# A message-passing kernel on Trainium2: POOL scatters three edge groups in a row, then gathers for all three

## The reference

```python
row, col = (edge_index[0], edge_index[1])            # src, dst; the edges are sorted by dst
edge_input = jnp.concatenate([x[row], x[col], edge_attr], axis=-1)
h = jax.nn.silu(edge_input @ eW1 + eb1)
m_ij = jax.nn.silu(h @ eW2 + eb2)
agg = jax.ops.segment_sum(m_ij, row, num_segments=x.shape[0])
node_input = jnp.concatenate([x, agg], axis=-1)
update = jax.nn.silu(node_input @ nW1 + nb1) @ nW2 + nb2
...
x = _layernorm(x + (x + update), axis=-1)
```

## Time and profile before

| what | us |
|---|---|
| median of 3 runs | 1586.3 (1585.7 to 1588.1) |
| the profiled execution, its own time | 1574.37 |
| its span | 1572.9 |
| POOL busy, of it scatters L540 (391) and gathers L497 (391) | 1041.8; 387.9 and 397.9 |
| PE busy | 1207.4 |
| DVE busy | 761.0 |
| ACT busy | 459.5 |
| DMA, moved in all | 352.94 MB, mean 224 GB/s |

### The profile page before, as it was taken

The page is one execution under the profiler, slowest core; times in us unless marked ns, Lnnn a source line. Parts: engine busy times, 40 slices in busy tenths (PEclk is TensorE's granted clock), DMA queues, the critical chain, the costliest instruction groups (busy, mean ns, idle before and its releaser), DMA issues.

```text
span 1572.9 us, 24119 instructions
## 1 busy us (share of the span) xinstructions
PE 1207.4 (77%) x6825; PEld 865.5 (55%) x6825; DVE 761.0 (48%) x2819; ACT 459.5 (29%) x846; POOL 1041.8 (66%) x1267
## 2 busy tenths in 40 slices
PE   3812677788787888878888877777778979999994
PEld 3711354555554555545545454544445569888884
DVE  8940343443434434344343333333333449888885
ACT  0000111222222222222222222211212247777774
POOL 8877466556565565555656565666566548999996
PEclk9985799899999999998999898989889889999998
DMA  9995444456666666566656556555545259999994
GB/s 376 410 408 204 123 126 140 145 172 200 183 185 190 186 195 182 186 192 181 192 177 200 170 172 183 172 172 172 165 147 176 62 197 410 412 412 413 410 408 167
DMA packets 175498, 352.94 MB, mean 224 GB/s; under 512 B 30350, under 2 KB 81855, under 8 KB 175364
## 3 DMA queue, kind: packets, MB, share of 16 engines
q1 hardware_dynamic: 128740, 230.97, 44.6%
q10 hardware_dynamic: 21600, 68.32, 10.9%
q0 software_dynamic: 25024, 52.10, 10.5%
HBM read 235.21 MB, written 116.06 MB: 223 GB/s over the span
## 4 chain that ended last, share of the span: by engine, by line
PE 35%; issue 23%; another core or an unknown queue 17%; POOL 12%; DVE 8%; SPq 2%; DMA 2%; POOLq 0%; ACT 0%; DVEq 0%
PE psum L659 10%; POOL windows L614 6%; PE psum L703 5%; PE psum L682 4%; PE psum L705 4%; PE psum L701 3%; PE psum L690 3%; PE psum L715 3%; PE psum L647 2%; DVE same L994 2%; DVE work L988 2%; DVE work L978 2%; POOL windows L594 2%; POOL windows L603 2%
## 5 line engine op out<-in xcount | busy, mean ns | idle before, releaser
L540 POOL DMA_INDIRECT table<-qs,pos x391 | 387.9, 992 | 346.9 <-DVE qs L1022 250.0
L497 POOL DMA_INDIRECT ring<-x_d,idx_src x391 | 397.9, 1018 | 128.0 <-issue 118.5
L659 PE MATMUL psum<-work,windows 128*128 128x128 f32 x1568 | 235.8, 314 | 158.7 <-issue 158.7
L659 PEld LDWEIGHTS psum<-work,windows 128*128 128x128 f32 x1568 | 224.8, 225 | 227.9 <-issue 227.9
L978 DVE COPY work<-psum 128x512 f32<-128x512 f32 x98 | 67.8, 692 | 515.6 <-remote 322.4
L733 PE MATMUL psum<-work,ring 128*128 128x80 f32 x1250 | 156.8, 280 | 27.6 <-DVE work L1042 24.1
L733 PEld LDWEIGHTS psum<-work,ring 128*128 128x128 f32 x1250 | 148.7, 195 | 37.1 <-issue 20.1
L703 PE MATMUL psum<-work,w_src 128*128 128x512 f32 x196 | 117.9, 685 | 48.3 <-DVE work L978 45.5
L1022 DVE COPY qs<-psum 128x512 f32<-128x512 f32 x98 | 67.6, 689 | 161.4 <-remote 150.7
L682 PE MATMUL psum<-xT_in,w_self 128*128 128x320 f32 x314 | 126.5, 487 | 24.8 <-issue 19.1
L785 ACT COPY u_out<-psum 128x320 f32<-128x320 f32 x129 | 55.0, 426 | 295.3 <-remote 250.6
(11 more groups left out here) (121 smaller groups left out, 1613.3 us busy)
## 6 DMA issues: line engine op xcount, KB each, us to landing
windows<-x_d SPq DMA_DIRECT2D x392, 128.0 KB
ring<-table SPq DMA_DIRECT2D x79, 528.0 KB, 11.0
table<-empty ACTq DMA_DIRECT2D x9, 4224.0 KB
edge_rows<-edges_dram SPq DMA_DIRECT2D x98, 384.0 KB
xT_in<-xT_d SPq DMA_DIRECT2D x78, 320.0 KB
out<-windows ACTq DMA_DIRECT2D x78, 320.0 KB, 6.1
u_dram<-u_out SPq DMA_DIRECT2D x64, 320.0 KB
own_x<-x_d SPq DMA_DIRECT2D x48, 320.0 KB, 8.5
```

The lines of the kernel that those rows point to most:

```text
L497: pool.indirect_dma_start(rows, None, x[:, :], bass.IndirectOffsetOnAxis(ap=idx[:, g * TILES + t:g * TILES + t + 1], axis=0)).then_inc(don ...
L540: pool.indirect_dma_start(table[:, :], bass.IndirectOffsetOnAxis(ap=pos[:, g * TILES + t:g * TILES + t + 1], axis=0), q[g % Q][:, t, :], None,
L659: last = nc.tensor.matmul(p_dst[:, t * P:(t + 1) * P], window[g % WINDOWS][:, t, r * D:(r + 1) * D], pick[g % 2][:, r, t * P:(t + 1) * P], ...
```

## The change

POOL's loop over groups goes in turns of TURN = 3: it scatters the three groups of the turn one after the other and then gathers all that is owed for the three. The condition of each scatter and each gather, their number and their buffers stay as they are. The other branch (`pool.Else()`), which runs for other inputs, is not touched.

```diff
 LEAD, SHORT = X_SRC + 2, 6
+TURN = 3
...
                 pool.wait_ge(s_fill, 16 * len(FILL_BLOCKS))
-                for g in range(GROUPS):
-                    scatter(g)
-                    for h in range(gathered_by(g, LEAD), gathered_by(g + 1, LEAD)):
+                for g in range(0, GROUPS, TURN):
+                    turn_end = min(g + TURN, GROUPS)
+                    for h in range(g, turn_end):
+                        scatter(h)
+                    for h in range(gathered_by(g, LEAD), gathered_by(turn_end, LEAD)):
                         gather_src(h)
```

## The result

| what | before | after |
|---|---|---|
| median of 4 runs each, us | 1586.0 (1572.4 to 1588.1) | 1621.8 (1620.2 to 1622.7) |
| ratio, 95% interval | | 1.0258 (1.0222 to 1.0294) |
| the profiled execution, us | 1574.37 | 1622.43 |
| span, us; mean granted clock of TensorE | 1572.9; 0.914 | 1621.0; 0.883 |

The change costs 2.6%. On the medians that is +35.8 us, on the two profiled executions +48.1 us; the difference is that the profiled execution of before stood 11.9 us under its median and that of after stands at its own.

What follows compares the result with a forecast made beforehand. It took the loop to be bound by waits, PE's signals being held while POOL issues gathers. Early turns +18, late +26, last +1 made +45 us: 1619 for the profiled execution, 1631 us on the median's scale, range 1568 to 1675.

Steps and rivals of the forecast that it cites:

- What bounds the kernel: Edge loop: PE's signals reach DVE late while POOL issues gathers, let through about 1.5 us after it stops.
- The rule set against it: On-chip memory: PE and ACT never wait, DMA never contends with compute engines; POOL's DMA order would change the time by 0.
- The first interval of a turn: POOL's burst of scatters and gathers plus 2.4 us idle: 17.4 us early; 19.9 + 2.4 us late.
- The second interval: Four scatters alone after PE's long stall: 9.0 us early, 11.0 us late, between bounds 7.3 and 13.08.
- The third interval: The last group of a turn, at full clock: 7.3 us.
- The sum: Turns of 33.7 us early (+18 in all) and 40.6 late (+26), +1 for the last gathering turn: +45 us.
- its signs of being right: Bursts of 14.9 and 19.9 us, 2.4 us idle, q copied 1.5 us after, low clock, late turns losing over half.
- The saving: Per turn, one burst's end of 2.4 us is paid instead of two; the clock takes it back.
- Faster: q gets through inside the new burst: turns of 31.9 us early, 37.0 late, about -25 us, 1561 us; chance 0.20.
- No change: The hold costs 5.1 us per gathered group however grouped, or POOL's order matters to no one: 1586 us; chance 0.12.
- Much slower: The hold grows with the run of gathers, 3 us more per turn: +90 on the forecast, 1720 us; chance 0.08.
- Late gathers: In four late turns PE waits for gathers, if the hold does not cover it: +26 us, 1657 us; chance 0.10.

Runs made afterwards that it cites:

- experiment 1: Kernel before, with the gathers of the edge loop left out (messages of groups 28 to 97 wrong): 1264.4 us in one run.
- experiment 4: Kernel before, but in each group POOL waits for q, then issues the gathers owed, then the scatters: 1566.5 us, ratio 0.9893.
- experiment 7: Changed kernel with one added wait: after a turn's first gathered group POOL waits for PE's next q matmuls: 1577.2 us, ratio 0.9987.
- experiment 11: Kernel before, with gathers spread tile by tile, three or four per group, after PE's q matmul signal and ahead of the scatters: 1508.4 us, ratio 0.9537.
- experiment 10: Changed kernel's order, turns of three, with POOL issuing plain DMAs of the same size in place of the loop's gathers: 1309.8 us in one run.
- experiment 2: Kernel before, with the edge loop's gathers replaced by plain DMAs of the same size issued by SP: 1304.7 us in one run.
- experiment 3: Kernel before, with the edge loop's gathers replaced by plain DMAs of the same size issued by POOL at the same places: 1268.2 us in one run.
- experiment 6: Changed kernel with the gathers kept nine groups ahead instead of six (SHORT = 9): 1621.7 us, ratio 1.0261.

## Why the prediction was right, and where its terms were off

The forecast was slower, 1631 us; 1621.8 was measured. By its own steps:

*What bounds the kernel.* Right for the loop. The length of POOL's unbroken work on indirect DMAs sets the period: shown by experiments 1, 4, 7 and 11, and experiment 10 shows that plain DMAs in their place don't hold. The 11 scatters at the kernel's end are an exception that the prediction doesn't cover. The rule set against it, in the Trainium skill's SBUF — State Buffer (Who interferes with whom), nearly holds for what it names, the traffic: 40 us of 320 with SP's loads (experiment 2), 4 with POOL's (experiment 3). It does not cover the signals: q is copied 9.9 us after PE has it.

*The first interval of a turn.* 17.4 us forecast early, 17.93 measured; 22.3 forecast late, 22.54 measured. The burst was as worked out, 14.9 and 19.9 us; the idle time behind it is 3.2 and 3.7 us in the turns shown and not 2.4, because PE's signals come 2.2 us after the end of a burst of 12 and not 1.5. The lower clock isn't needed for it: behind the burst that ends at 482.08 us the clock was full (PEclk 1.00), and POOL idled as long,

```profile
482.08:485.27 3.19, 1.36 (x4) 0.29 (x2) 0.93 (x3) 0.86 (x2) 0.00 (x1) 1.00 0.17 48
```

```profile
485.28 0.99 POOL L541 DMA_INDIRECT table<-qs,pos  x1 [3.19 <-DVE qs L1025]
```

What sets the 2.2 us stays open.

*The second interval.* 9.0 early and 11.0 late were forecast, 7.92 and 9.06 measured. The late value was midway to the 13.08 us of the earlier trace rows, and that was a mis-reading: the interval from 1039.61 us is not four scatters alone, it has a burst of 8,

```profile
1044.80 0.99 POOL L497 DMA_INDIRECT ring<-x_d,idx_src  x1 [0.30 <-issue]
```

until 1049.56 us, so it shows a gathering group and says nothing on the clock's price for four scatters. The clock does fall, on the mean for 4.4 us of this interval early and 6.3 us late. The longest, 11.3 us, came once.

*The third interval.* 7.3 us was forecast as PE's own pace; 8.06 early and 8.22 late were measured. This step was mis-read too. PE's own pace with the node part is 8.21 us, as experiment 1 shows with no gathers at all; the 7.32 us in the earlier trace rows is, as I read it, a group in which PE had work done ahead during the hold.

*The sum.* A turn of 33.9 us early (746.0 / 22) against 33.7 forecast, 39.8 late (318.6 / 8) against 40.6: +23 and +19 us where +18 and +26 stood, +4 at the end for +1, and +1.6 before the first scatter for nothing. The total, +48 against +45, is better than its terms, and that is luck: the second interval was too long, and the first and the third were too short. Late turns make 40% of the loss, where the prediction had put more than half among its signs of being right. On the medians it is +36 us; the scale of the prediction added the 11.9 us by which the execution of before was low, and that of after was not. Between profiled executions the forecast was 3 us too low (1619 against 1622.4); the added 11.9 us turned that into 9 too high.

*The saving.* I wrote that one burst's end is paid for instead of two and that the clock takes it back. The runs give a plainer account, an estimate from their means: against PE's pace of 8.05 us, a burst of 9.9 us loses about 4.3 us (12.34 − 8.05) and one of 14.9 us 9.9 us (17.93 − 8.05). So some 5 to 5.6 us of a burst are free, and each DMA beyond costs about its 1.25 us. Before used the free piece of each burst that held gathers, two per early turn and three per late one; the change uses one per turn, and four scatters alone (4.8 us) never exceed theirs. By this and without the clock a late turn would go from 3 × 12.35 = 37.1 to 2 × 8.05 + 22.3 = 38.4 us (measured 37.4 and 39.8); the rest I put down to the lower clock. It was not tested at other lengths than 7, 8, 12 and 16 DMAs, and the scatters at the kernel's end don't follow it.

*The rivals.* Faster (q gets through inside the burst): no early or late turn of three did so; it happened once, in the last turn, at 1278.4 us. In one late turn POOL idled only 0.94 us behind the burst (1163.56 us). No change: the interval excludes it, and experiment 7 undoes the cost without moving a DMA out of its turn. Much slower: the idle time behind a burst grows from 2.4 to 3.7 us, not by 3 us more. Late gathers: PE's waits for their landing, which the prediction had among its signs of being wrong, are there, 25.7 us, but covered, as the prediction had it (experiment 6); experiment 10 shows such waits bare.

*The clock.* It falls where PE stands still during a burst, and it goes with the cost: 290 us at the lower level against 177.5. With the break of experiment 7 it is 188 us and the time is before's. How much of the 36 us is clock and how much is PE standing still these runs don't separate.

**What stays open.** What inside the chip holds PE's signals while POOL issues indirect DMAs, and why one comes through in mid-burst; why the 11 scatters at the end hold nothing (SP issues no loads beside them, which no run has tried in the loop); why the signals come later behind a longer burst; why turns with a break are 2 us longer late than worked out.

## What to carry to other kernels

Where a producer's signal and its consumer's start stand several us apart and the profile calls the releaser "remote", look at what POOL issues meanwhile: here, in most steps of the loop, a consumer of PE's results was late when POOL issued indirect DMAs for more than about 5 us without a break. An engine with idle time is not free of cost. What paid in this kernel was to start such DMAs on an earlier signal (3.1% faster) and to spread them evenly over the steps as well (4.6% in all); to collect them made it 2.6% slower. A short wait put in the middle of a long run of issues paid for itself.

## What the runs showed of the chip that was not expected

- The loop's 279 gathers cost 320 us, more than a microsecond each, though no engine is full; with plain DMAs of the same bytes on POOL in their place the kernel is 316 us faster.
- Four plain DMAs take POOL 2.2 us to issue, four indirect ones 5.0 us (0.94 to 1.02 us each and 0.30 us between them); eight plain ones in the middle of a burst of 14.6 us held no signal (experiment 10).
- Only PE's signals were late. DVE's and ACT's came within 0.01 us in the same edge phase.
- SP's issue of four window loads, 3.98 us beside scatters and 5.97 beside before's gathers, is 9.00 us in the change's burst:

```profile
646.38 9.00 SPq L410 DMA_DIRECT2D windows<-x_d  x4
```

- The hold covers signals of PE to POOL itself: in experiment 7 the wait for PE's semaphore ends 1.8 us after POOL's last DMA, in experiment 11 1.7 us after, though the profile shows no work of PE ending then ("remote").
